# Gelu of the gate ahead of the square root on ScalarE, in a four-layer attention and gated-recurrence kernel

## What is computed

```python
def _hawk_block(x, ...):
    xn = _rmsnorm(x, gamma1)
    z = xn @ W_in.T
    gate, xc = (z[..., :HID], z[..., HID:])            # HID = 256
    xc = causal_conv_4_taps(xc) + conv_b
    g = xc @ W_gates.T + b_gates
    forget, inp = (g[..., :HID], g[..., HID:])
    alpha = jnp.exp(-8.0 * softplus(forget_base) * sigmoid(forget))
    beta = jnp.sqrt(1.0 - alpha ** 2 + 1e-06)
    xs = beta * sigmoid(inp) * xc
    h = _linear_recurrence(alpha, xs)                  # h[t] = alpha[t] * h[t-1] + xs[t]
    x = x + gelu(gate) * h @ W_out.T
    gz = _rmsnorm(x, gamma2) @ W_grow.T
    mgate, mx = (gz[..., :GHID], gz[..., GHID:])       # GHID = 256
    return x + gelu(mgate) * mx @ W_shrink.T
```

## Time and profile before

| | |
|---|---|
| median of 3 runs | 1532.55 us (1526.43, 1532.55, 1537.96) |
| profiled execution, own time | 1527.02 us |
| its span | 1525.2 us |
| mean granted TensorE clock | 0.929 of full speed |
| second phase | from about 980 us of the span to the end |
| loads of tables on the gate gelu's line L880 | 15 x 1.283 us |

### The profile page before, as it was taken

One profiled execution on the slowest core, in us unless ns is written; L12 is line 12 of the kernel. 1 busy time (PEld: TensorE's weight loads), 2 busy tenths in 40 slices (PEclk: granted clock), 3 DMA queues, 4 the chain that ended last, 5 costly groups with the idle time before them and its releaser, 6 DMA issues.

```text
span 1525.2 us, 29278 instructions
## 1 busy us (share of the span) xinstructions
PE 1213.6 (80%) x8528; PEld 495.7 (33%) x8528; DVE 1232.6 (81%) x2629; ACT 961.3 (63%) x1621; POOL 840.0 (55%) x1051
## 2 busy tenths in 40 slices
PE   1388988998898899898899998547878877788862
PEld 0022222232232233233232232213445434444532
DVE  2578889899799799799799895453898899889863
ACT  1067767777687677677677778345765665676630
POOL 4224346555555555555556543634676676766663
PEclk9999989999999999999999999677999999999975
DMA  1233023022103103203202200000000000000000
GB/s 37 29 88 50 17 35 50 16 36 51 36 18 50 37 17 50 46 9 51 52 2 51 33 13 2 1 1 0 1 12 11 7 7 14 7 7 15 8 8 21
DMA packets 47021, 37.88 MB, mean 25 GB/s; under 512 B 8080, under 2 KB 44816, under 8 KB 46864
## 3 DMA queue, kind: packets, MB, share of 16 engines
q1 hardware_dynamic: 42256, 29.65, 10.5%
q0 software_dynamic: 4608, 6.32, 2.6%
HBM read 6.04 MB, written 4.19 MB: 7 GB/s over the span
## 4 chain that ended last, share of the span: by engine, by line
PE 31%; DVE 25%; issue 16%; POOL 11%; DMA 5%; SPq 5%; ACT 4%; DVEq 1%; POOLq 0%; ACTq 0%
PE bank L197 9%; DVE neg_max L484 8%; PE bank L178 8%; DMA k_stack<-k_parts 4%; SPq L617 4%; PE bank_pair L165 4%; DVE probs L1027 3%; ACT probs L341 3%; PE bank L206 2%; PE bank L267 2%; DVE probs L897 2%; PE bank L719 1%; POOL probs L1135 1%; POOL rs_x L1069 1%; PE bank_pair L711 1%
## 5 line engine op out<-in xcount | busy, mean ns | idle before, releaser
L484 DVE TENSOR_REDUCE neg_max<-bank_pair 128x2 f32<-128x1024 f32 x512 | 609.9, 1214 | 96.9 <-PE bank_pair L165 95.0
L341 ACT ACTIVATE probs<-bank 128x512 f32<-128x512 f32 x1024 | 557.1, 595 | 162.1 <-PE bank L178 132.0
L178 PE MATMUL bank<-q_stack,k_stack 50*128 50x512 bf16 x1024 | 362.8, 400 | 27.6 <-issue 13.6
L197 PE MATMUL bank<-probs,v_pad 128*32 128x256 f32 x4096 | 343.7, 408 | 9.1 <-issue 8.6
L165 PE MATMUL bank_pair<-k_stack,q_stack 48*128 48x512 bf16 x1024 | 300.3, 407 | 58.1 <-DMA k_stack<-k_parts 32.3
L178 PEld LDWEIGHTS bank<-q_stack,k_stack 50*128 50x128 bf16 x1024 | 82.7, 94 | 294.6 <-ACT probs L341 232.8
L711 PE MATMUL bank_pair<-probs,w_gates 128*128 128x512 f32 x256 | 130.9, 659 | 17.0 <-DVE probs L1027 14.1
L197 PEld LDWEIGHTS bank<-probs,v_pad 128*32 128x32 f32 x4096 | 83.8, 110 | 183.3 <-issue 181.0
L1027 DVE SCALAR_TENSOR_TENSOR probs<-v_pad,conv_w,probs 128x512 f32<-128x512 f32 x96 | 98.1, 1061 | 6.3 <-ACT probs L861 5.6
L711 PE MATMUL bank_pair<-probs,w_in 128*128 128x512 f32 x128 | 67.2, 651 | 31.3 <-ACT probs L861 28.5
L1135 POOL TENSOR_TENSOR probs<-probs 128x1024 f32<-128x1024 f32 x16 | 37.7, 2359 | 89.7 <-DVE probs L1049 89.7
(11 more groups left out here) (224 smaller groups left out, 2208.4 us busy)
## 6 DMA issues: line engine op xcount, KB each, us to landing
q_stack<-q_parts SPq DMA_DIRECT2D x192, 64.0 KB
k_stack<-k_parts POOLq DMA_DIRECT2D x96, 64.0 KB, 4.6
k_stack<-k_parts SPq DMA_DIRECT2D x96, 64.0 KB
x_all<-in_z_dram SPq DMA_DIRECT2D x16, 256.0 KB, 2.8
out_dram<-x_all SPq DMA_DIRECT2D x16, 256.0 KB, 2.3
q_stack<-max_rows SPq DMA_DIRECT2D x64, 8.0 KB
w_gates<-in_w_gates_dram SPq DMA_DIRECT2D x1, 512.0 KB, 3.7
w_in<-in_w_in_dram SPq DMA_DIRECT2D x1, 256.0 KB, 2.7
```

Of the source, the lines that this page charges most:

```text
L178: nc.tensor.matmul(st_ps[h][:, :], k_stack[par][rows, p, c * P:(c + 1) * P], q_stack[par][rows, p, :], start=True, stop=True).then_inc(s[" ...
L197: mm = nc.tensor.matmul(acc[32 * g:32 * g + 32, cols], v_pad[bpar][:, kc, 4 * a + g, :], probs[:, (a % 2) * 4 * C + g * C + kc, cols], sta ...
L341: nc.scalar.activation(probs[:, (p // 2 % 2) * 4 * C + (2 * (p % 2) + h) * C + c, :], st_ps[h][:, :], ACT.Exp, scale=SCALE).then_inc(s["ex ...
L484: nc.vector.tensor_reduce(neg_max[j // 4][:, c, j % 4, :], score_ps[c % 2][:, :, :], AX_X, ALU.max, negate=True).then_inc(s["max_read"], 1)
```

## The change

In `scalar`, the block that takes the gelu of the gate moves up past the square root and the copy of h4T. Its waits (for the gate product and for gh of block i-2) move with it. Nothing else is changed.

```diff
@@ -865,6 +865,10 @@
             wait(act, s["mg_ps"], b + 1)
             wait(act, s["shrink_ps"], b)
             A(grown, pair1[:, :, :], ACT.Gelu).then_inc(s["mg_ready"], 1)
+        if live(i, 0):
+            wait(act, s["gate_ps"], i + 1)
+            wait(act, s["gh_ready"], i - 1)
+            A(gate_g[par], pair0[:, :, :], ACT.Gelu).then_inc(s["gate_ready"], 1)
         if live(i, -1):
             b = i - 1
             wait(act, s["om_ready"], b + 1)
@@ -874,10 +878,6 @@
             wait(act, s["h4T_ps"], b + 1)
             wait(act, s["y_ps"], b)
             A(h4T, bank_t[:, :], ACT.Copy).then_inc(s["h4T_ready"], 1)
-        if live(i, 0):
-            wait(act, s["gate_ps"], i + 1)
-            wait(act, s["gh_ready"], i - 1)
-            A(gate_g[par], pair0[:, :, :], ACT.Gelu).then_inc(s["gate_ready"], 1)
```

## The result

The changed kernel takes 1537.3 us (median of 20 runs, 1531.4 to 1545.0), the kernel before 1531.9 us (median of 20, 1526.4 to 1538.0). The ratio is 1.0034, with a 95% interval of 1.0019 to 1.0049: some 5 us slower, where 4.0 were forecast, and within 1%. The profiled execution has a span of 1531.2 us against 1525.2.

The account below looks back on a forecast made before the run. VectorE and, through `gh`, GpSimd and TensorE were taken to pace a block, not ScalarE. Terms 2.84 + 1.12 + 0 gave +4.0 us on the median 1532.55, so 1536.5 us, range 1528 to 1543.

Parts of the forecast that it names:

- The removed loads: ScalarE's gate line (L880): 15 table loads, 19.2 us, go but gain 0, since ScalarE idles 7.86 us afterwards.
- Beta's cover in the middle: Iteration 8: beta comes 2.15 us later, but L1045 needs it only at 1231.60, leaving 3.4 us; cost nothing.
- The h4T copy: Middle iterations: the copy, queued behind the sqrt, runs a microsecond later, yet the forget product starts as before; cost nothing.
- the rival's mechanism: Middle iterations: late h4T copy delays L735, L740, forget product and L719; 16.6 us slower in all, 1549.1; chance 0.05.
- Iteration 1: Second phase, L1045: the sqrt behind the gate gelu makes it 2.84 us late, and this reaches the end.
- Iteration 2: Second phase: L1045 comes 1.27 us late, of which 1.12 us pass through GpSimd into iteration 3.
- GpSimd takes on the 1.27 less 0.15: Iteration 2, GpSimd: L1093 had waited only 0.15 us, so the rest of the delay passes on, +1.12 us.
- Iteration 3: Sqrt would end at 1085.35 against L1045 at 1086.08: 0.7 us of cover, price 0.
- in iterations 1 and 2 and nowhere else: Sign of a right forecast: L1045 late after the taps in those two iterations only.
- The load at L815: Iterations 2 and 3: the load most likely only moves ahead of the tanh, 0; other end 2.6 us more.
- The middle: Middle iterations: spacing of L1045 from block to block unchanged; no cost.
- The sum: Whole kernel: 2.84 + 1.12 + 0 = +4.0 us, with ends +2.4 and +6.6; 0.26% slower.

Follow-up runs that it names:

- two-load run: Changed kernel with two more table loads between gate gelu and sqrt in every iteration from 4 to 15; 1547.3 us, ratio 1.0104 to the kernel before.
- the run with six loads: Changed kernel with six more table loads between gate gelu and sqrt in iteration 1 alone; 1546.7 us, ratio 1.0101 to the kernel before.
- the sqrt early: Kernel before, with the sqrt put ahead of the tanh of inp in iteration 2 and the gelu set loaded there; 1529.4 us, ratio 0.9967.

## Why the prediction was right, and where not

**The removed loads, priced at 0.** Right, and shown: with 12 of them gone and the start left alone there is no difference (0.9986). In place of the 15 loads, 19.2 us of work, ScalarE now waits longer: 15.6 us more before the exp and its load, and 21.5 us in all before the gate gelu, where it was 3.9. The Trainium skill's rule of grouping activations by table set ("ScalarE: Activation LUTs", "Table sets: the hidden batching unit") does save the loads here, and saves no time, since ScalarE isn't what the next step waits for.

**Beta's cover in the middle, 3.4 us forecast in iteration 8.** Measured 3.27, and L1045 waits for beta in no iteration from 4 on. Right.

**The h4T copy, 0 forecast.** Right for the change: no forget product is late. But I named too large a margin for it. I counted on the forget product's 3.70 us and 2.5 us until `gh`; in iteration 11 of both kernels this product takes 5.40 us, which leaves 0.8 us, and in iterations 7 and 13 of both it starts late, right behind L740, which leaves 0.5. The nearest place is iteration 4 of the kernel after, where I had counted 0.4 us and 0.13 were left. The two-load run shows that the rival's mechanism is real and begins somewhere short of 2.6 us more. What I had down for that run as the slack that matters, beta's 2.6 us, wasn't the nearest one.

**Iteration 1, 2.84 us forecast.** The start of L1045 relative to the entry moved by 2.49 us in the profile after, by 2.8 to 2.9 in four other kernels with this order and no loads added there. In the kernel after, the four gate matmuls took 3.15 us instead of the 3.56 that I took over from before. Right, and the run with six loads shows that it goes through to the end one for one.

**Iteration 2, 1.12 us forecast.** The gap is 1.24 (1.27 forecast). From L979 of iteration 2 to L1045 of iteration 3 the new order costs 1.55 us in the profile after and 1.6 to 2.5 in five others: the term was too small. The step that failed is the one behind the gap: "GpSimd takes on the 1.27 less 0.15". L1093 waited for VectorE, 0.46 us, and not for GpSimd's own queue, because L719 had become slower. Its 16 matmuls took 2.89 us, and up to 3.78 in the others, where they had taken 1.95. From iteration 1 to 3 as a whole the profile after shows only 0.75 us, since 0.8 were won ahead of L979: iteration 2's inp product took 5.03 us instead of 5.84. That is not the order's doing; with iteration 1 changed, this product took 4.74 to 6.08 us, and with the old order there 4.54 to 5.84.

**Iteration 3, 0 forecast, with 0.7 us of cover.** Wrong. L1045 waits 0.34 us for beta in the kernel after, and 0.34 to 0.35 in three of the four others with the new order there: the gate product ended 3.3 us before the taps did, where I had 4.2 from the profile before. And the sign that I gave, late "in iterations 1 and 2 and nowhere else", doesn't hold.

**The load at L815, 0.** Right: the two loads moved, and none was added.

**The middle, +1.20 us in the profile after.** 0.90 of it lie between iterations 4 and 5, where L719 takes 3.22 us instead of 2.05, at a granted clock of 0.60 instead of 1.00. This is not a cost of the order in the middle: with the new order from iteration 4 on and the old one before, the stretch is as it was (28.31). But it goes with the order at the start. The five kernels with the new order in iteration 3 have 29.1 to 30.7 us there (the highest has two loads more from iteration 4 on), the five without it 28.3. So it looks like a further cost of the first iterations, some 0.9 us that I had at nothing. That iteration 3 is its cause was not tried by itself, and each kernel has one profile. The rest of the middle, and the 1.5 us at the entry, are spread: the entry lies anywhere from 1009.7 to 1018.2 us, and nothing ahead of it differs.

**The sum.** It was 4.0, and the ratio gives 5.2 us (2.9 to 7.5). With what the profile after shows by place, 2.49 in iteration 1, 1.55 in iteration 2 and 0.90 behind iteration 3, the order costs 4.9. So the place and the mechanism of the two main terms were right, the second was too small and the third was missing. The interval holds 4.0 as well as 4.9, so the times alone don't show the difference.

**Open.** The two-load run lies 10.7 us above the changed kernel by the ratios; its ledger shows 4.7 of them in the middle and 4.1 after iteration 15, where its code is the same. Its matmuls there are longer (the last shrink product takes 3.75 us instead of 2.02). Why they are was not tried.

## What to carry to other kernels

Before regrouping activations to save table loads, look at what the engine does after the last instruction of the group: if it waits there, a saved load becomes a longer wait, and only what is pushed back inside the group counts. Look at the first and last turns of a software pipeline by themselves: the cover of the middle comes from other blocks' work that isn't there yet. And of a step that is moved back, follow every consumer and its queue, since the nearest limit may be an in-order engine two steps behind a copy, not the consumer one thinks of.

## What the runs showed of the hardware

Work that TensorE gets done sooner can make its next work slower. The view of windows for iteration 2; columns are the stretch, its length, busy time (instructions) of PE, PEld, DVE, ACT, POOL, the granted clock of TensorE, DMA share and GB/s. First before:

```profile
1055.00:1061.00 6.00, 3.70 (x8) 1.44 (x8) 5.48 (x8) 5.94 (x6) 0.00 (x0) 1.00 0.00 0
1061.00:1066.50 5.50, 5.34 (x10) 2.34 (x11) 3.35 (x3) 0.01 (x1) 3.18 (x2) 0.69 0.00 0
1066.50:1070.00 3.50, 3.50 (x33) 3.40 (x31) 1.58 (x6) 3.41 (x5) 3.42 (x6) 1.00 0.02 5
```

then after:

```profile
1063.00:1066.70 3.70, 3.68 (x8) 1.44 (x8) 2.46 (x3) 2.38 (x2) 0.00 (x0) 1.00 0.00 0
1066.70:1070.30 3.60, 0.02 (x1) 0.00 (x0) 2.22 (x2) 3.51 (x5) 2.41 (x2) 1.00 0.00 0
1070.30:1073.20 2.90, 2.90 (x17) 2.90 (x18) 0.00 (x0) 0.21 (x1) 2.82 (x5) 0.67 0.00 0
```

Before, the forget product came late and fell into a stretch with a mean granted clock of 0.69, part of it at the lower level (1.2 GHz); L719, which followed without a pause, ran at 2.4 GHz. After, the forget product was early and at full clock, TensorE was idle for 3.6 us, and the clock that it was granted in the 2.9 us after that was 0.67: L719 took 2.89 us instead of 1.95. All six kernels with the new order in iteration 2 show the same: 3.58 or 3.59 us idle, then a granted clock of 0.50 to 0.67 and 2.89 to 3.78 us for L719. The three with the old order there have 1.00 and 1.95 us. With the sqrt early, TensorE was idle for 2.23 us, and L719 took 2.05 us at 1.00. It is L719, not the forget product, that the next step waits for. Where these stretches fall differs from kernel to kernel and also between kernels with the same order: from iteration 1 to 3 the new order took 68.07, 67.79, 70.10, 70.09 and 70.11 us. That is as large as the effect of the order itself, and a profile of one execution can't separate the two without a ledger that cuts fine enough.
